# Expert matrices split in the list steps instead of once ahead, and listed rows turned by VectorE

## The reference

```python
# layer 0: grouped convolution over the last axis + context, then
base_out = einsum('bsi,oi->bso', x, base_w) + base_b
res_hidden = einsum('bsi,ri->bsr', x, A)              # 64 ranks
topw, topi = top_k(softmax(x @ router_w.T), 2)         # 16 experts, 2 chosen
delta = einsum('bse,bsr,eor->bso', combine, res_hidden, B)   # B: 16 x 1024 x 64
return base_out + delta * 0.5
# layer 1: per-sample 64 x 64 channel mix chosen by attention, then
out = x @ base_W.T + (gated rank-8 products of 28 experts, 2 chosen)
x = x + layer0(x);  x = x + layer1(x)
```

## Time and profile before

| | us |
|---|---|
| median of 3 runs | 1207.8 |
| the three runs | 1205.23, 1207.8, 1211.32 |
| the profiled execution | 1200.46 |
| its span | 1198.5 |
| PE busy | 1171.6 |
| ACT busy | 767.6 |
| DVE busy | 706.4 |
| POOL busy | 297.5 |

### The profile page before, as it was taken

The page is one execution under the profiler, slowest core; times in us unless marked ns, Lnnn a source line. Parts: engine busy times, 40 slices in busy tenths (PEclk is TensorE's granted clock), DMA queues, the critical chain, the costliest instruction groups (busy, mean ns, idle before and its releaser), DMA issues.

```text
span 1198.5 us, 22055 instructions
## 1 busy us (share of the span) xinstructions
PE 1171.6 (98%) x6783; PEld 1034.3 (86%) x6783; DVE 706.4 (59%) x1985; ACT 767.6 (64%) x1746; POOL 297.5 (25%) x315
## 2 busy tenths in 40 slices
PE   6999999999999999999999999999999999999998
PEld 6999999999899999898787787787788888888887
DVE  6677778777465655557764444454445555555552
ACT  5566667666586776864667767767645665755751
POOL 4111733323222223234312112111131222222200
PEclk9999999999999999999999999999999999999999
DMA  9566566775999999979699999999875455455410
GB/s 333 185 241 258 191 225 229 285 268 165 253 319 327 311 322 311 325 269 242 127 245 304 268 293 311 281 292 299 269 165 118 99 123 110 118 123 118 110 53 36
DMA packets 84698, 267.15 MB, mean 223 GB/s; under 512 B 23248, under 2 KB 27472, under 8 KB 77360
## 3 DMA queue, kind: packets, MB, share of 16 engines
q1 hardware_dynamic: 72608, 230.12, 58.4%
q0 software_dynamic: 11600, 36.06, 17.0%
q10 hardware_dynamic: 432, 0.30, 0.1%
HBM read 154.24 MB, written 112.20 MB: 222 GB/s over the span
## 4 chain that ended last, share of the span: by engine, by line
PE 41%; DMA 7%; SPq 1%; issue 1%; DVE 1%; ACT 1%; POOL 0%; ACTq 0%; POOLq 0%; DVEq 0%
PE z L1461 12%; PE z L1462 12%; PE z L1463 12%; DMA ht<-hs_dram 3%; DMA xin<-zs_dram,gpos 2%; DMA xin<-x_dram 1%; PE c L1461 1%; PE c L1463 1%; PE c L1462 1%; PE c L1528 1%; PE prep L1725 1%; DMA x<-zs_dram,gpos 1%; DVE xb L1433 1%; PE c L1532 1%; PE c L1530 1%
## 5 line engine op out<-in xcount | busy, mean ns | idle before, releaser
L754 ACT ACTIVATE moved<-mid 32x256 f32<-32x256 f32 x944 | 392.2, 415 | 139.0 <-DVE mid L1023 114.6
L1461 PE MATMUL z<-w_1h,yh 128*128 128x384 f32 (+1 forms) x512 | 190.0, 371 | 0.0
L1461 PE MATMUL z<-w_0h,yh 128*128 128x384 f32 (+1 forms) x512 | 187.4, 366 | 0.2 <-DVE xb L1433 0.2
L1463 PE MATMUL z<-w_1l,yh 128*128 128x384 f32 (+1 forms) x512 | 185.8, 363 | 0.0
L1463 PE MATMUL z<-w_0l,yh 128*128 128x384 f32 (+1 forms) x512 | 185.8, 363 | 0.0
L1462 PE MATMUL z<-w_1h,yl 128*128 128x512 f32 (+1 forms) x504 | 183.0, 363 | 0.0
L1462 PE MATMUL z<-w_0h,yl 128*128 128x512 f32 (+1 forms) x504 | 182.8, 363 | 0.0
L669 POOL TENSOR_TENSOR carrier<-ones_col 128x1 f32<-128x1 f32 x96 | 25.5, 266 | 539.1 <-DVE den L1117 131.8
L1461 PE MATMUL z<-w_2h,yh 128*128 128x336 f32 (+1 forms) x512 | 152.9, 299 | 2.1 <-DVE yl L1031 2.1
L1463 PE MATMUL z<-w_2l,yh 128*128 128x336 f32 (+1 forms) x512 | 152.5, 298 | 0.0
L1462 PE MATMUL z<-w_2h,yl 128*128 128x252 f32 (+1 forms) x504 | 149.9, 297 | 0.0
(11 more groups left out here) (217 smaller groups left out, 2587.8 us busy)
## 6 DMA issues: line engine op xcount, KB each, us to landing
bd<-bd_dram SPq DMA_DIRECT2D x96, 512.0 KB, 9.0
zs_dram<-zt SPq DMA_DIRECT2D x96, 512.0 KB, 10.2
hs_dram<-zt SPq DMA_DIRECT2D x34, 512.0 KB, 6.6
x8raw<-in_x_dram SPq DMA_DIRECT2D x32, 516.0 KB, 4.4
xin<-in_x_dram SPq DMA_DIRECT2D x32, 512.0 KB, 6.9
x_dram<-xb SPq DMA_DIRECT2D x32, 512.0 KB, 5.2
out_dram<-xb SPq DMA_DIRECT2D x32, 512.0 KB, 4.7
bd_dram<-bd SPq DMA_DIRECT2D x8, 1024.0 KB, 6.5
```

Source lines behind the costliest of these rows:

```text
L754: return nc.scalar.activation(o, i_, ACT.Copy)
L1461: T.matmul(o, ah, wh, start=start, stop=False, **kw)
L1463: return T.matmul(o, ah, wl, start=False, stop=stop, **kw)
```

## The change

The split of the expert matrices ahead of the lists is taken out: no `load_b`, `b_high`, `b_low`, `store_b`, and no `bd_dram`. A list step loads the raw matrices (64 x 1024 instead of 64 x 2048 for each v) and splits them itself: ACT `bd_high(s, j)` and DVE `bd_low(s, j)`, one of each for each pair. The raw buffer and the low part share their memory. In layer 0, ACT does pair 0 at the end of the step before, ahead of `ht_high`, and pair 1 at its step's start, ahead of `moves`; DVE does both right behind `conv_out`. In layer 1, ACT does pair 0 ahead of `exps` and pair 1 ahead of the outputs; DVE does pair 0 first in the step and pair 1 behind its block transposes.

The hidden rows are loaded as blocks: two transfers for each listed tile, each of 32 partitions x 4 x 32 columns, in runs of 128 bytes instead of 256. One DVE block transpose of 128 x 256 in 32 x 32 blocks (`ht_turn`) then gives what PE's two transposes gave, and `ht_high` and `ht_low` read it from SBUF.

```diff
-            def load_b(p, w):
-                sp.dma_start(braw[w][:, :], b0_pair[p]).then_inc(b_in[w], 16)
-            def store_b(p):
-                sp.wait_ge(b_lo, p + 1)
-                sp.dma_start(bd_dram[p], bd[0][:, :, :].bitcast(F32)).then_inc(bd_out, 16)
...
             def load_ht(s, w, first=False):
                 if not first:
-                    sp.wait_ge(ht_ps, s)
+                    sp.wait_ge(ht_done, s)
                 for v in range(PER):
                     at = sp.value_load(tab_row[0:1, PER * s + v, :], ...)
-                    sp.dma_start(ht[v // 2][:, ranks(v)], hs_t[w][at]).then_inc(ht_in[v], 16)
+                    for i in range(R0 // Q):
+                        p = R0 * (v % 2) + Q * i
+                        sp.dma_start(ht[p:p + Q, v // 2, :, :], hs_q[w][at, :, :, Q * i:Q * (i + 1)]).then_inc(ht_in[v], 16)
...
-                sp.dma_start(bd[v // 2][ranks(v), :, :].bitcast(F32), bd_of[e]).then_inc(bd_in[v], 16)
+                sp.dma_start(bdraw[v // 2][ranks(v), :], b0_in_order[e]).then_inc(bd_in[v], 16)
...
+            def bd_high(s, j):
+                for v in (2 * j, 2 * j + 1):
+                    act.wait_ge(bd_in[v], 16 * s + 16)
+                copy(bdh[j][:, :], bdraw[j][:, :]).then_inc(bd_hi, 1)
...
             def ht_high(s, first=False):
-                act.wait_ge(ht_ps, s + 1)
+                act.wait_ge(ht_done, s + 1)
...
+            def bd_low(s, j):
+                dve.wait_ge(bd_hi, 2 * s + j + 1)
+                V.tensor_tensor(bdl[j][:, :], bdraw[j][:, :], bdh[j][:, :], ALU.subtract).then_inc(bd_lo, 1)
...
+            def ht_turn(s):
+                for v in range(PER):
+                    dve.wait_ge(ht_in[v], 16 * R0 // Q * (s + 1))
+                V.transpose(ht_turned[:, :, :].rearrange("p j (q r) -> p j q r", r=Q), ht[:, :, :, :]).then_inc(ht_done, 1)
...
-            def turn_ht(s, first=False):
-                for v in range(PER):
-                    pe.wait_ge(ht_in[v], 16 * s + 16)
...
             def listed_pair(s, j):
                 pe.wait_ge(hl_ready, s + 1)
-                for v in (2 * j, 2 * j + 1):
-                    pe.wait_ge(bd_in[v], 16 * s + 16)
+                pe.wait_ge(bd_lo, 2 * s + j + 1)
```

More of the change, by code:

```diff
@@ L169, in build @@
         moved = sb(ctx, "moved", [P, L])
[L170 to L175, removed]
+        bdh, bdl, bdraw = zip(*(split_pair(ctx, f"bd{j}", [2 * R0, L]) for j in range(PER // 2)))
+        ht = sb(ctx, "ht", [P, PER // 2, P // Q, Q])
+        ht_turned = sb(ctx, "ht_turned", [2 * R0, PER // 2, P])
         hh = sb(ctx, "hh", [2 * R0, PER // 2, P], F32R)
@@ L494, in _, with step0 @@
             load_x(0, 1)
-            def step0(i, u, first=False, lists=None, more=True, start=False, clear=None, split=None):
+            def step0(i, u, first=False, lists=None, more=True, start=False, clear=None):
                 t = 2 * i + u
@@ L547, in _ @@
             for t in range(12, NA):
-                step0(t // 2, t % 2, clear=(1, (t - 12) * parts // 4, (t - 11) * parts // 4),
-                      split=(11, 1, False) if t == 12 else None)
+                step0(t // 2, t % 2, clear=(1, (t - 12) * parts // 4, (t - 11) * parts // 4))
             i = NA // 2
@@ L871, in mixed_out, with step0 @@
                     nc.scalar.activation(o, v, ACT.Identity, bias=mbrow[:, :]).then_inc(a1.c_out[b], 1)
-            def step0(t, u, first=False, split=None, w1_piece=None, lists=False, first_list=False, turn=None):
+            def step0(t, u, first=False, w1_piece=None, lists=False, first_list=False, turn=None):
                 s = t - S0_LISTS
                 turned = exists(t + 1) and not first
+                if lists:
+                    bd_high(s, 1)
                 if turned:
@@ L898, in step0 @@
                     y_high(a0, t + 1, 1 - u)
-                if split is not None:
-                    b_high(*split)
                 if lists:
@@ L908, in _ @@
                 step0(t, t % 2, first=t == 0)
-            for u in range(2):
-                step0(4 + u, u, split=(2, u))
-            with act.Fori(3, 6) as i:
+            with act.Fori(2, 6) as i:
                 for u in range(2):
-                    step0(2 * i + u, u, split=(i, u))
+                    step0(2 * i + u, u)
             step0(12, 0)
@@ L955, in step1 @@
                     w1_high(1, w1_pieces(1)[0:2])
+                if lists:
+                    bd_high(s, 0)
                 exps(a1, t)
@@ L1275, in residual, with step0 @@
                 V.tensor_tensor(o, z[b][:, 0:w.stop - w.start], o, ALU.add).then_inc(a0.z_out[b], 1)
-            def step0(i, u, w, first=False, split=False, w1_piece=None, tables=False, places=False, turn=None):
+            def step0(i, u, w, first=False, w1_piece=None, tables=False, places=False, lists=False, turn=None):
                 t = 2 * i + u
@@ L1287, in step0 @@
                         conv_out(t + 1)
-                    if split:
-                        b_low(t - 1, 1 - u)
+                    if lists:
+                        for j in range(PER // 2):
+                            bd_low(t - S0_LISTS, j)
                     if at(t, 3):
@@ L1317, in step0 @@
                     tiles_of_lists(0)
+                if turn is not None:
+                    ht_turn(turn)
                 rank0(t, u, w)
@@ L1403, in step1 @@
                     turn_rows(a1, tiles)
+                    if lists:
+                        bd_low(s, 1)
                 dve.wait_ge(a1.hT_hi, t + 1)
@@ L1668, in step0 @@
                     rank(t, w)
-                if turn is not None:
-                    turn_ht(turn, first=at(turn, 0))
                 if exists(t + 2):
```

95 lines of the change are left out of this document (33 added, 62 removed).

## The result

| | before | after |
|---|---|---|
| median of 11 timed runs each, us | 1207.8 | 1218.8 |
| their range | 1202.5 to 1211.6 | 1213.2 to 1220.8 |
| ratio of the two, 95% interval | | 1.009, 1.007 to 1.011 |
| the profiled execution | 1200.46 | 1220.19 |
| its span | 1198.5 | 1218.4 |

The forecast was 1201.3 us with a range of 1192 to 1215. The changed kernel lies above the range.

The account below looks back on a forecast made before the run. PE was taken as the bound, busy 98%, with the DMA engines also full in layer 0's list steps. Terms summed to -4.1 us, plus 2.4 us of DMA relief: 1207.8 to 1201.3 us, range 1192 to 1215.

Parts of the forecast that it names:

- part 4: Layer 0's steady list step: the split's copies and subtractions and the doubled ht transfers stay hidden, cost 0.
- part 1: Two PE transposes leave each of 24 list steps, 0.17 us per pair: -4.1 us.
- part 5: Stretch before the lists: without the split's copies and subtractions PE waits less for x8's low part, -0.8 us.
- part 3: First list step of layer 0: PE waits for a longer chain to pair 0's low part, +2.6 us.
- the relief of the DMA queue: Saturated stretches: a third of the 7.3 us between profiled execution and median goes, 2.4 us.
- The slower rival: Layer 0 list steps: pair 1's load lands late, ScalarE's copy holds the moves; 1216.7 us at 8 us latency; chance 0.18.
- Part 2: Waits for ht go from PE to DVE, four of the five in layer 1: -2.6 us.
- Part 6: First list step of layer 1: DVE and ACT 2 us late through pair 0's second load, +0.8 us.

Follow-up runs that it names:

- shared: The changed kernel with SyncE reading one table instead of two per listed tile, the expert's number worked out from the row's; 1205.1 us, ratio to before 0.999.
- half_bd: The kernel before with only the matrices' half: raw matrices loaded and split in the list steps, hidden rows as before; 1204.8 us, ratio 0.999.
- half_ht_shared: The kernel before with only the hidden rows' half of the change, plus one table read instead of two per listed tile; 1206.4 us, ratio 1.000.
- before_spread: The kernel before with GpSimd scattering three of six held-back tiles between the residual additions of tiles 6 and 7; 1203.0 us, ratio 0.997.
- before_look: The kernel before, unchanged, run once more for a second profile; one run, 1211.0 us.
- shared_first: The changed kernel with one table read instead of two and pair 0's matrices issued ahead of the hidden rows; 1204.0 us, ratio to before 0.998.
- first_spread: shared_first with GpSimd scattering three of six held-back tiles between the residual additions of tiles 6 and 7; 1197.2 us, ratio to before 0.991.

## Why the prediction was wrong, step by step

**The step that failed** is in part 4: "I expect 4 to 5 us for the second load, issued 1.2 us later than now". The latency was right, even a little better, under 3.9 us; the issue came 4.5 us later in the step (1.1 instead of 5.6 us ahead of the convolution's sum). I had counted the added issues once, as a delay of the first load, and never laid SyncE's row of a whole step beside TensorE's 18.9 us. The views for that were at hand: in the row before shown above, SyncE pauses 2.6 us and is busy for the rest; four transfers more take 2.0 of it (0.50 us each in SyncE's records). The remainder goes to what no view of before showed: in 325:525 a table read takes 0.48 us on average where it took 0.38, eight times a step, and the issues of `xin` and `x8raw` 0.76 and 0.66 us where they took 0.36 and 0.35. Without four of the reads, in shared, the steady steps gained 2.0 us. So part 4's cost, which I put at 0, was 10.7 us against shared in the first profile, where the steps as a whole lost 8.7; over two profiles of each kernel they lost 6.6, so part 4 cost 8.6 beside part 1's gain of 2.0.

**The miss added up.** Over two profiles of each, the changed kernel lost 12.1 us where the sum had a gain of 4.1. Of these 16.2 us part 4 makes 8.6, steps 7 to 10 with part 5's missing gain 5.9 (5.1 + 0.8), and part 3 1.7 (4.3 against 2.6). Layer 1 came out 1.0 better than forecast, and 0.9 lie in the other steps. The 2.4 us that I let go with the relief of the DMA queue didn't show in the medians.

**The slower rival** named the right place, ScalarE's copy of pair 1 at the head of the step, with the wrong cause, a load that lands late. It had "SP's own row gets 1.5 us longer" only as an argument on the side. Its 1216.7 us was the nearest of all figures, which is luck: it had 13 us in these steps and nothing for steps 7 to 10.

**Part 1** was right: 0.02 us between place count and convolution, and 0.18 us a step gained in the kernels whose SyncE has room (2.0 us in 11 steps of shared). **Part 2** had the right amount by the wrong way: PE has no wait on `ht`, and layer 1 won 3.9 and 4.0 us in the two profiles of after, where 4.1/2 + 2.6 = 4.6 was the sum of parts 1 and 2. But half_bd, where PE still turns the rows and waits for them itself, won 2.4 of it and has no such wait there either. So what took it away was the emptier DMA queue (share 0.83 in layer 1's list steps of half_bd, 1.01 in those of half_ht_shared), and not the hand-over to VectorE: half_ht_shared, which has the hand-over alone, lost 1.8 us there.

**Part 3** was the right mechanism, mis-sized: +4.5 and +4.2 instead of +2.6. Against the ledger's 10.4 us at step 17, PE started pair 0 at 322.86 - 10.4 = 312.5 where I had 311.4. SyncE issued the eight in 5.59 us, not 5.1, and pair 0's two loads at 313.52 and about 314.8, 2 us later behind the first `ht` than before, not 1.5. The second landed 3.8 us later, not 3. PE waited 6.5 us, and the next 4 us had a granted clock of 0.50, against 0.57 before. The 299.1 us of that part is 302.02 - 2.91 in the earlier trace rows, and 1.7 of its +2.6 us stand for a lowered clock behind the wait: no run shows that term by itself. Of the 4.5 us in the first profile 2.0 were lost by pair 0's start (312.5 against 310.43) and about 2.5 behind it.

```profile
307.17 5.59 SPq L436 DMA_DIRECT2D ht<-hs_dram  x8
313.52 1.79 SPq L442 DMA_DIRECT2D bd0raw<-in_b_dram  x2
...
318.57 1.06 ACT L728 ACTIVATE bd0h<-bd0raw 128x1024 fp32r<-128x1024 f32 x1 [9.64 <-DMA bd0raw<-in_b_dram]
...
322.86 0.76 PE L1500 MATMUL c<-bd0h,hh 64*128 64x512 f32 x1 [6.46 <-DVE bd0l L1111]
```

**Part 5** failed too: it held no term for what else stands in that stretch. Taking out the split ahead brought no 0.8 us in steps 4 to 12; steps 7 to 10 of them lost 5.1 us more than before, by a stall that no row of before showed. Even the wait that I shared out was not the split's: the 1.5 us at 160 us, most of the 2.5, are gone in before_spread, which keeps the split. **Part 6** was small, as forecast: +0.5 and +0.6 us in that step, and made good in the next.

**The relief of the DMA queue** took place: 0.76 to 0.80 instead of 1.02. It also did what I had guessed of it: the timed runs of half_bd and shared spread over 3.4 and 4.8 us, where before's, on the same chips, spread over 11 to 14. Room on SyncE alone doesn't do it: half_ht_shared has more of it than half_bd (26.4 us of 200), but a DMA share of 1.02, and spreads over 10.6 us. In the sum it came to nothing, since the same steps gave the time away on SyncE's row. How much of the 7.3 us between profile and median lies there stays open: before_look has 4.5 of its 10.5 us in those steps, before_spread none of its 4.8.

## What to carry to other kernels

Before adding transfers to a loop, write down the issuing engine's whole row for one step, waits and table reads included, and compare its length with the step's: here the issue itself of a 16 KB transfer took SyncE 0.32 us in the changed kernel, and that of a 512 KB one 0.35 to 0.5 us in the kernel before. An engine that issues and isn't listed as busy can be the bound all the same; its sign here was that the load followed above landed in under 3.9 us and ScalarE waited 29.0 us in 200 for pair 1's loads nevertheless. One profile of a kernel that scatters by 1% is no base for a sum of single microseconds: take a second one before dividing the difference.

## What the runs showed of the hardware that was not expected

A read of one table value on SyncE took from 267 to 1071 ns in the step shown, 0.48 us on average in 325:525 against 0.38 in the kernel before; leaving out four in a step took the median from 1218.8 to 1205.1, 1.0% by the ratios. The issue of the same 512 KB load, `xin`, took 0.36 us on average in the kernel before and 0.76 in the changed one. Beside an unbroken row of 14 scatters on GpSimd VectorE stood still for 7.2 us in the changed kernel and TensorE paused twice, for 1.1 and 0.7 us, and moving three of the six held-back tiles' scatters 13 us ahead took what PE lost there from 3.7 us (shared_first) to none (first_spread).
